# Weights of a ternary feed-forward read and prepared beside the last batch of a 16-head attention, in one program per engine

## The reference

```python
x = x + _L0_xattn_ref(ctx, ctx, _layernorm(x), mask_Bx1x1xS2, Wv, bv, Wk, bk, Wq, bq, Wo, bo)   # 16 heads of 32
x = x + _L0_ffn_ref(_layernorm(x), w_gate, w_up, w_down)                                        # ternary, 2048 inner
x = x + _L1_xattn_ref(_layernorm(x), ctx, mask_BxS2, ln_g, ln_b, Wq, Wkv, Wo)                   # 8 heads of 64
x = x + _L1_ffn_ref(_layernorm(x), w_gate, w1, w2, w3, sw1, sw2, sw3, expert_bias)              # routed, 8 experts

def _weight_quant(w):
    scale = 1.0 / jnp.clip(jnp.mean(jnp.abs(w)), 1e-05)
    return jnp.clip(jnp.round(w * scale), -1.0, 1.0) / scale
def _act_quant(x):
    scale = 127.0 / jnp.clip(jnp.max(jnp.abs(x), axis=-1, keepdims=True), 1e-05)
    return jnp.clip(jnp.round(x * scale), -128.0, 127.0) / scale
def _bitlinear(x, w):
    return jnp.einsum('bsi,oi->bso', _act_quant(x), _weight_quant(w))
gate = jax.nn.silu(_bitlinear(x, w_gate)); up = _bitlinear(x, w_up)
return _bitlinear(gate * up, w_down)
```

## Time and profile before

| | |
|---|---|
| median of 3 runs | 2240.57 us (2238.35 to 2241.69) |
| profiled execution | 2243.0 us, span 2241.3 us |
| mean granted TE clock | 0.963 of 2.4 GHz |
| 16-head attention ends | about 693 us |
| first `turn_h` of the feed-forward | 777.47 us |
| last output add of the feed-forward | 1142.91 us |
| 8-head attention, routed feed-forward | to the end of the span |

### The profile page before, as it was taken

One profiled execution on the slowest core, in us unless ns is written; L12 is line 12 of the kernel. 1 busy time (PEld: TensorE's weight loads), 2 busy tenths in 40 slices (PEclk: granted clock), 3 DMA queues, 4 the chain that ended last, 5 costly groups with the idle time before them and its releaser, 6 DMA issues. The chain is left out here.

```text
span 2241.3 us, 47529 instructions
## 1 busy us (share of the span) xinstructions
PE 2065.7 (92%) x14976; PEld 1581.7 (71%) x14976; DVE 1286.5 (57%) x3831; ACT 1075.6 (48%) x2781; POOL 780.2 (35%) x1435
## 2 busy tenths in 40 slices
PE   5999999999993699999958999999999799999986
PEld 4888888888872444444437888888888678888744
DVE  4667667667662677777736656565655433333354
ACT  4776776767764544444424444444444322222134
POOL 2544554545543566666522122222221112111100
PEclk8999999999996799999978999999999999999999
DMA  5111212111005122222140121212120382222100
GB/s 171 53 42 51 70 41 80 40 50 71 19 30 221 47 71 70 70 66 63 59 161 31 39 77 38 76 38 76 38 76 19 114 281 77 78 84 70 66 1 0
DMA packets 91368, 158.31 MB, mean 71 GB/s; under 512 B 11248, under 2 KB 21488, under 8 KB 90752
## 3 DMA queue, kind: packets, MB, share of 16 engines
q1 hardware_dynamic: 91264, 157.10, 20.5%
HBM read 123.50 MB, written 33.57 MB: 70 GB/s over the span
## 5 line engine op out<-in xcount | busy, mean ns | idle before, releaser
L402 POOL TENSOR_SCALAR a_probs<-a_probs,a_rinv 128x256 f32<-128x256 f32 x512 | 237.6, 483 | 300.6 <-DVE a_rinv L628 300.6
L489 ACT ACTIVATE a_probs<-a_probs,a_negm 128x256 f32<-128x256 f32 x512 | 254.7, 501 | 126.9 <-DVE a_negm L612 126.2
L402 POOL TENSOR_SCALAR c_probs<-c_probs,c_rinv 128x256 f32<-128x256 f32 x128 | 67.2, 535 | 392.4 <-DVE c_rinv L628 392.4
L612 DVE CUSTOM_DVE_ANT_0 a_probs<-a_s,a_mbias 128x256 f32<-128x256 f32 x512 | 191.6, 417 | 10.8 <-PE a_s L879 10.7
L621 DVE COPY a_pT<-a_pt 128x512 f32<-128x512 f32 x128 | 88.4, 691 | 167.8 <-PE a_pt L896 167.7
L1203 ACT ACTIVATE b_raw<-b_g,b_xs 128x512 f32<-128x512 f32 x128 | 88.1, 688 | 184.0 <-PE b_g L1374 159.3
L896 PE MATMUL a_pt<-a_ident,a_probs 128*128 128x128 f32 x1024 | 158.1, 278 | 16.2 <-POOL a_probs L402 6.8
L489 ACT ACTIVATE c_probs<-c_probs,c_negm 128x256 f32<-128x256 f32 x256 | 127.4, 502 | 90.3 <-DVE c_negm L612 90.3
L896 PEld LDWEIGHTS a_pt<-a_ident,a_probs 128*128 128x128 f32 x1024 | 124.3, 143 | 36.3 <-issue 13.0
L1286 DVE SCALAR_TENSOR_TENSOR b_raw<-b_u,b_xs,b_raw 128x512 f32<-128x512 f32 x128 | 96.1, 751 | 66.9 <-PE b_u L1374 37.9
L1374 PE MATMUL b_g<-b_wg,b_raw 128*128 128x512 bf16 x512 | 132.4, 381 | 1.4 <-ACT b_raw L1194 1.4
(11 more groups left out here) (296 smaller groups left out, 4711.7 us busy)
## 6 DMA issues: line engine op xcount, KB each, us to landing
m_ew<-in_L_ffn_w_dram SPq DMA_DIRECT2D x24, 512.0 KB, 8.8
a_cbuf<-in_ctx_dram SPq DMA_DIRECT2D x16, 512.0 KB, 5.1
a_xbuf<-in_x_dram SPq DMA_DIRECT2D x16, 512.0 KB, 4.2
a_resb<-in_x_dram SPq DMA_DIRECT2D x16, 512.0 KB, 3.7
x<-a_resb SPq DMA_DIRECT2D x16, 512.0 KB, 2.8
b_xbuf<-x SPq DMA_DIRECT2D x32, 256.0 KB, 2.7
b_raw<-x SPq DMA_DIRECT2D x32, 256.0 KB, 2.7
x<-b_raw SPq DMA_DIRECT2D x32, 256.0 KB, 2.0
```

Of the source, the lines that this page charges most:

```text
L402: last = nc.gpsimd.tensor_scalar(pr, pr, rinv[:, s, r:r + 1], 0.0, ALU.mult, ALU.add)
L489: nc.scalar.activation(pr, pr, ACT.Exp, bias=negm[:, s, h % 2, t:t + 1], scale=-1.0, accum_out=ssum[:, s, QT * (h % 2) + t:QT * (h % 2) + ...
L612: nc.vector.tensor_tensor_reduce(out=probs[:, s, h % 2, t], in0=s_bank[h][:, t * SEQ:(t + 1) * SEQ], in1=mbias[:, el.par], scale=-sm_scale ...
```

## The change

`a` and `b` become one block: each engine runs the program of `a` and then that of `b`, with no common end between them. All tensors get fixed places in SBUF, so that buffers of `b` lie where those of `a` are no longer used; `gone` names for each place the semaphore and count after which it is free. The eight PSUM banks are shared by name. Hooks in the attention program (`beside`) carry part of the preparation into its last two batches:

- SyncE reads gate and up during the last but one batch, as places come free, and down at the end of the last; the first two row tiles of x1 too.
- ScalarE's six Abs passes over gate and up go behind quarters 2 and 3 of the last but one batch and 0 and 1 of the last; `integers` of gate behind quarters 2 and 3. VectorE's share of the sums goes behind the last quarter of the last but one batch and behind quarter 1 of the last, each time waiting for ScalarE's three. TE adds them (`total`) in quarters 0 and 2 ahead of the scores.
- GpSimd rounds one slice behind each pair of heads (gate in quarters 0 and 1, most of up in 2 and 3), and normalises the first two tiles.
- TE turns the first half of gate in quarter 3, behind heads 2 and 3.
- The rest follows attention: the second half of gate, up, and, beside tiles 0 and 1, the down weights. The turned weights use two banks in place of three; the integers of a matrix use one buffer of four slices, written again when it was turned. `xround` is gone: the rounded x is written over the normalised x. `o0` and `o1` of the last batch use two free score banks.

Both attentions get the fixed places (`oT` is single for 16 heads); nothing else in `c` and `m` changes. The core of the diff (most of the rest is a change of indentation; `scale` and `total` are as before but for the bank, cut in two with `magnitude_sum`):

```diff
-    with ExitStack() as ctx:
-        def sb(name, shape, dt=F32):
-            return ctx.enter_context(nc.sbuf_tensor(f"{tag}_{name}", shape, dt))
+    def sb(name, at, shape, dt=F32):
+        return nc.alloc_sbuf_tensor_at(f"{tag}_{name}", shape, dt, offset=SB_BASE + at)
...
+    def bank_of(el, u):
+        if u in BEHIND and last_batch(el):
+            return s_bank[BEHIND.index(u)]
+        return x_bank[units.bank(u, el)]
...
+    gone = {"x": (xn_ready, batches * QT), "context": (x_done, units.count(ALL, "tc1", last)),
+            "xn": (x_done, units.count(ALL, "tx1", last)), "wv": (x_done, units.count(ALL, "v1", last)),
+            "wk": (x_done, units.count(ALL, "k1", last)), "wq": (x_done, units.count(ALL, "q1", last)),
+            "even q, k": (s_done, (batches - 1) * QUADS * S_SETS), "odd q, k": (s_done, batches * QUADS * S_SETS),
+            "scores": (ttr_done, batches * heads * QT), "probs": (pt_done, batches * heads),
+            "pT": (pv_done, batches * GROUPS), "o_bank": (otlo_done, batches * GROUPS),
+            "work banks": (out_done, (batches - 1) * QT), "all": (out_done, batches * QT)}
+    made = {"rows": stored}
...
+            if beside and last_batch(el.plus(1)):
+                beside.sync_beside(sp)
...
+        if beside:
+            beside.sync_behind(sp)
...
+                if beside and last_batch(el):
+                    beside.gpsimd_beside(pool, 2 * q)
+                for m in (range(2) if QUADS == 2 else range(1)) if nq > 0 or el.has(1) else ():
+                    norm_probs(ne, nq, m)
+                if beside and last_batch(el):
+                    beside.gpsimd_beside(pool, 2 * q + 1)
...
+                if beside and last_batch(el.plus(1)):
+                    beside.scalar_beside(act, q - QUADS)
+                if beside and last_batch(el):
+                    beside.scalar_beside(act, q)
...
+            probs_out(el, q, 0)
+            if beside and last_batch(el):
+                beside.vector_totals(dve, q)
+            recip(el, q, 1)
...
+                if beside and last_batch(el.plus(1)):
+                    beside.vector_beside(dve, q - QUADS)
+                if beside and last_batch(el):
+                    beside.vector_beside(dve, q)
...
+                for j in range(4):
+                    transpose_probs(el, q, j)
+                    if j == 0 and beside and last_batch(el):
+                        wait_for(pe, otlo_done, el.n * GROUPS + q - 1)
+                        beside.tensor_totals(pe, q)
+                    if j == 0 and (nq > 0 or el.has(1)):
+                        scores(ne, nq)
+                    if j == 0 and beside and last_batch(el):
+                        beside.tensor_totals_read(pe, q)
...
+                    if beside and last_batch(el):
+                        beside.tensor_beside(pe, q, j)
...
-        raw = sb("raw", [P, 3, WN])
-        tern = sb("tern", [P, 3, WN], BF16)
+    raw = [[sb(f"raw{n}_{c}", (at + 8 * c) * KB, [P, SN]) for c in range(SLICES)] for n, at in enumerate((0, 32, 132))]
+    wg = sb("wg", 64 * KB, [P, KC, inner], BF16)
+    wu = sb("wu", 80 * KB, [P, KC, inner], BF16)
+    xbuf = sb("xbuf", 96 * KB, [P, 2, DIM])
+    tern = sb("tern", 100 * KB, [P, SLICES, SN], BF16)
+    wd = sb("wd", 116 * KB, [P, IK, DIM], BF16)
+    g_bank, u_bank = [banks[3], banks[7]], [banks[6], banks[1]]
+    tx_bank, th_bank, d_bank = banks[2][:].bitcast(BF16), [b[:].bitcast(BF16) for b in banks[4:6]], banks[0]
...
+    def load_slice(sp, n, c):
+        view = (w_gate, w_up, w_down)[n].rearrange("(t p) c -> p t c", p=P)
+        cut = view[:, :, c * DIM:(c + 1) * DIM] if n == 2 else view[:, 4 * c:4 * c + 4]
+        sp.dma_start(raw[n][c][:].rearrange("p (t c) -> p t c", c=DIM), cut).then_inc(w_loaded[n][c], 16)
...
+    def sync_beside(sp):
+        sp.wait_ge(*prior.gone["x"])
+        load_slice(sp, 0, 0)
+        sp.wait_ge(*prior.gone["context"])
+        load_slice(sp, 0, 1)
+        sp.wait_ge(*prior.gone["wv"])
+        load_slice(sp, 0, 2)
+        load_slice(sp, 0, 3)
+        sp.wait_ge(*prior.gone["even q, k"])
+        load_slice(sp, 1, 0)
+        load_slice(sp, 1, 1)
+        sp.wait_ge(*prior.gone["wk"])
+        load_slice(sp, 1, 2)
+        load_slice(sp, 1, 3)
...
+    def sync_behind(sp):
+        sp.wait_ge(w_abs_act, 2 * (SLICES - 1))
+        sp.wait_ge(prior.made["rows"][0], 16)
+        for el in first[:2]:
+            load_x(sp, el)
+        sp.wait_ge(*prior.gone["probs"])
+        load_slice(sp, 2, 0)
+        load_slice(sp, 2, 1)
+        sp.wait_ge(*prior.gone["pT"])
+        load_slice(sp, 2, 2)
+        load_slice(sp, 2, 3)
...
+    def gpsimd_beside(pool, step):
+        if step < 4:
+            rounded(pool, 0, [step])
+        elif step == 5:
+            rounded(pool, 1, [0])
+        elif step >= 6:
+            normalise(pool, first[step - 6])
+            rounded(pool, 1, [step - 5])
...
-                for n in range(3):
-                    wait_apart(pool, w_scale, 3 * n + 3)
+        rounded(pool, 1, [3])
+        quantise_x(first[0])
+        quantise_x(first[1])
+        normalise(pool, first[2])
+        rounded(pool, 2, range(SLICES))
+        quantise_h(first[0])
...
+    def magnitudes(act, n, cs, other):
+        for c in cs:
+            act.wait_ge(w_loaded[n][c], 16)
+            wait_for(act, w_abs_act, n * (SLICES - 1) + c)
+            nc.scalar.activation(other, raw[n][c][:], ACT.Abs, accum_out=wsum[:, n, c:c + 1]).then_inc(w_abs_act, 1)
...
+    def integers(act, n, cs):
+        for c in cs:
+            act.wait_ge(w_rounded, n * SLICES + c + 1)
+            wait_for(act, w_turned, (n - 1) * 2 * HALF + (c // 2 + 1) * HALF if n > 0 else 0)
+            nc.scalar.activation(tern[:, c], raw[n][c][:], ACT.Copy, bias=-MAGIC).then_inc(w_integer, 1)
...
+    def scalar_beside(act, quad):
+        rows_place = xbuf[:].rearrange("p a d -> p (a d)").bitcast(BF16)
+        if quad == -2:
+            act.wait_ge(*prior.gone["xn"])
+            magnitudes(act, 0, [0], rows_place)
+        elif quad == -1:
+            magnitudes(act, 0, [1, 2], rows_place)
+        elif quad == 0:
+            magnitudes(act, 1, [0, 1], rows_place)
+        elif quad == 1:
+            magnitudes(act, 1, [2], rows_place)
+        elif quad == 2:
+            act.wait_ge(*prior.gone["odd q, k"])
+            integers(act, 0, [0, 1])
+        elif quad == 3:
+            integers(act, 0, [2, 3])
...
-                magnitudes(0)
-                magnitudes(1)
-                integers(0)
-                magnitudes(2)
-                integers(1)
-                integers(2)
+        integers(act, 1, range(SLICES))
+        act.wait_ge(*prior.gone["pT"])
+        magnitudes(act, 2, range(SLICES - 1), spare[:])
...
+            if el.n == 0 if isinstance(el.n, int) else False:
+                silus(el.plus(1), [0])
+                integers(act, 2, [0, 1])
+                silus(el.plus(1), [1])
+                integers(act, 2, [2, 3])
+                silus(el.plus(1), range(2, NC - 1))
+            elif el.has(1):
+                silus(el.plus(1), range(NC - 1))
...
+    def magnitude_sum(dve, n):
+        last = SLICES - 1
+        dve.wait_ge(w_loaded[n][last], 16)
+        nc.vector.tensor_reduce(wsum[:, n, last:last + 1], raw[n][last][:], AX.X, ALU.add,
+                                apply_absolute_value=True).then_inc(w_abs_dve, 1)
+        dve.wait_ge(w_abs_act, (n + 1) * last)
+        dve.wait_ge(w_abs_dve, n + 1)
+        nc.vector.reduce_sum(wpart[:, n:n + 1], wsum[:, n], AX.X).then_inc(w_part, 1)
...
+    def turned(dve, numbers):
+        for i in numbers:
+            dve.wait_ge(w_turned, i + 1)
+            nc.vector.tensor_scalar(turns[i][1], th_bank[i % 2][:], 1.0, -1.0, ALU.min, ALU.max).then_inc(w_out, 1)
...
+    def vector_totals(dve, quad):
+        if quad in (0, 2):
+            scale(dve, quad // 2)
...
+    def vector_beside(dve, quad):
+        if quad == -1:
+            magnitude_sum(dve, 0)
+        elif quad == 1:
+            magnitude_sum(dve, 1)
+        elif quad == 2:
+            row_stats(dve, first[0])
+            row_stats(dve, first[1])
+        elif quad == 3:
+            turned(dve, range(HALF))
...
+                if isinstance(el.n, int) and el.n == 0 and c == 1:
+                    scale(dve, 2)
+                if isinstance(el.n, int) and el.n == 1 and c == 2:
+                    turned(dve, range(4 * HALF, len(turns)))
...
-                scale(0)
-                scale(1)
-                turned(0)
-                scale(2)
-                turned(1)
+        x_scale(dve, first[0])
+        turned(dve, range(HALF, 2 * HALF))
+        x_scale(dve, first[1])
+        turned(dve, range(2 * HALF, 4 * HALF))
+        row_stats(dve, first[2])
+        magnitude_sum(dve, 2)
+        hidden(first[0], steady=False)
...
+    def turn(pe, numbers):
+        for i in numbers:
+            n, _, src = turns[i]
```

(49 more changed lines are left out.)

2051 lines of the change are left out of this document (1007 added, 1044 removed).

## The result

The changed kernel took 2224.78 us (median of 4 runs, 2222.8 to 2225.59), the kernel before 2241.13 beside it (4 runs, 2238.35 to 2242.14). The ratio is 0.9928, 95% interval 0.9911 to 0.9945: faster by 0.72%. The forecast was 2225.

A forecast was written before the change was run, and what follows sets the result against it. TensorE was busy 92%, so gains lay where it idled between attention and feed-forward. Attention ending +12.0, the way to the first `turn_h` -29.7 and low clock +2.0 gave -15.7: from 2243.0 to 2227.3, as median 2225, range 2210 to 2236.

The forecast's parts named there:

- 1, the wait for the third Abs pass: Quarter 0 of the last batch: VectorE's sum over gate waits for ScalarE, so scores start later, +5.3 us.
- 2, low clock behind it: Quarter 0 of the last batch: after idling, TensorE starts at the low clock level, +2.0 us.
- 3, the wait for the sixth pass: Quarters 1 to 2 of the last batch: sixth Abs pass, sum and total delay the scores, +2.5 us.
- 5, 6, 7, integers, turns, own banks: Late last batch: integer passes of gate +0.9, four turns between heads +2.2, last output projection's own bank -0.85 us.
- E to T: From attention's end (E) to the first `turn_h` (T): 54.6 us for 84.25, so -29.7.
- first `turn_h` at the low clock: Tile 1 of the feed-forward: TensorE has idled again and pays the low clock once, +2.0 us.
- Reads and GpSimd (4): Beside the last batch: no reader waits for data; GpSimd's roundings of 1.95 us fall in its waits, costing nothing.
- the rival in which the two block each other: GpSimd's seven passes each hold up VectorE for their length, 13.7 us lost: 2238.6 us; chance 0.05.
- ScalarE unbroken from there for 14 us: Sign after attention's last add: ScalarE runs without a break for 14 us while TensorE waits for the turned x.
- The gaps left out: Waits between the turns: two gaps of some 2 us each, uncounted; by the clock rule the result would be near 2229.
- Changes only its places, which I count as nothing: The 8-head attention changes only its places in memory and banks, counted as 0 us.
- Slower by the shared buffer of x: Tile loop: quantised x made in place adds a wait paid 32 times; at 0.7 us a tile, 2247 us; chance 0.05.

The follow-up runs named there:

- the run with everything behind: Changed kernel with every piece of preparation put behind the attention instead of beside its last two batches: 2252.0 us, ratio 1.0052.
- all four edits: Changed kernel with both sums late, Abs passes over down behind the turned x, down clamps split: 2209.85 us; with old 8-head places too, 2208.47 us.

## Why the prediction was right

The mechanism was as it said. That the total was right to 0.2 us is luck: single terms were off by up to 3 us, and they cancelled. Step by step, in its numbers:

| step | predicted | in the profile after |
|---|---|---|
| before the last batch | 0 | +2.2 |
| 1, the wait for the third Abs pass | +5.3 | +5.4 |
| 2, low clock behind it | +2.0 | +1.2 (1.1 to 2.3 in seven profiles) |
| 3, the wait for the sixth pass | +2.5 | +2.4 |
| 5, 6, 7, integers, turns, own banks | +2.25 | -0.9 |
| E to T | -29.7 | -30.95 |
| first `turn_h` at the low clock | +2.0 | 0 |
| the rest of the program | 0 | +3.2 |
| sum | -15.7 | -17.4 |

- *Reads and GpSimd (4).* No reader waited for a slice beside the batch for more than 0.2 us, and GpSimd's seven passes took 1.98 to 1.99 us each, and VectorE's reduction of 128x2048 at 672.52, with one of them under way from 673.94, 2.28 (2.29 before): the rival in which the two block each other is out.
- *Waits 1 and 3* were right in place and size, and the runs with late sums took them away. The passes come 2.1 us apart and not 1.9, since each ends with a read of its accumulator of 0.19.
- *Steps 5 to 7* were mis-sized. By the run with everything behind, the own banks bring 1.6 from the scores of quarter 3 to E, not 0.85 (27.3 to 25.6). Integers and turns cost the difference of the changed kernel to that run, 26.4 - 25.6 = 0.8 (up to 1.5 in the other six profiles with both sums early), not 3.1. The reasons are argued, not tried apart: the turns found TensorE waiting for the heads, and with them the clock was back at 1.00 from 690 on, 13 us ahead of E, while before it stood at 0.50 until 686, 7 us ahead of E.
- *E to T.* Turned x predicted for E+14.2, measured +13.8; the columns took 6.56 for 5.5; the sum over down +27.1 for +28.2; T +53.3 for +54.6. "ScalarE unbroken from there for 14 us" was wrong: it first waited 4.96 us at 707.07, until TensorE had turned the slice whose buffer it overwrites. That wait was counted, as the four turns ahead of it, but under another name. Two terms do not follow from the prediction's own rate of 0.85 a turn: four turns of up are 3.4 and not 4.2 (2.7 in the profile), and the x scale of 1.3 with four turns is 4.7 and not 4.0; they nearly cancel.
- *The clock price of the first `turn_h`* was not paid in the changed kernel, nor with the Abs passes moved, where `turn_h` came 7.8 us or more earlier (1.05 us for its transposes in both), but in the three kernels with split clamps (1.5 us). There the turns of down come in short pieces with waits of up to 2.5 us, and the granted clock is 0.50 to 0.57 at `turn_h`; with the clamps in a row the turns run almost without a break after one wait of 6.06 us and the clock is back at 1.00 before it. The Trainium skill, "TensorE: Matmul & The Clock Gate", section "HAM oscillation — how this bites in real kernels", has the price paid per gap. The traces agree in part: both pairs of columns ran low, 717 to 724 and 731 to 737, but with all four edits the same waits lowered the clock in one kernel and not in the other. The gaps left out cost little, as the forecast took it: the turns of down ran at 0.61 (748 to 756), but hidden between VectorE's clamps, and the turns behind E ran at 0.53 in the first profile and at 1.00 in its repetition, with the turned x only 0.2 us apart (E+13.2 and E+13.0), since the Abs passes held it in both.
- *"Changes only its places, which I count as nothing"* failed: the first attention is 1.1 to 1.8 us longer and the second 1.4 to 2.3, and weight loads take 190 and 191 ns in place of 188, 96 times a batch. In `c` putting the places back took away the longer loads and 0.8 to 1.7 us; in `a` it is argued from the same longer loads. That the loads are what costs the time is not shown: 3 ns on 1440 loads of `c` would be 4.3 us, more than is lost.
- *Slower by the shared buffer of x:* 357.87 us over 31 tiles before, 358.32 after, 0.015 a tile. Out.

The price of the waits was thus taken rightly from rows, and what the terms missed, -7.3 and +5.5, cancelled by luck: the range, not the middle, is what the working could promise.
